# Expert shares from one tanh, routing in smaller pieces, ten gather buffers, and a different order of softmax steps in a decoder layer on one core

## The reference

```python
x = x + attn(layernorm(x), ...)            # 16 heads of 16, rotary, layernorm of q and k
x = x + xattn(layernorm(x), ctx, ...)      # 16 heads, low-rank queries, latent context of 64
x = x + ffn(layernorm(x), Wr, Wg, Wu, Wd)

def ffn(x, Wr, Wg, Wu, Wd):                # 8 experts of width 256, the best 2 for each token
    probs = softmax(x @ Wr)
    topk_w, topk_idx = top_k(probs, 2)
    topk_w = topk_w / sum(topk_w)
    return sum over experts i of w_i * ((silu(x @ Wg[i]) * (x @ Wu[i])) @ Wd[i])
```

## Time and profile before

| what | value |
|---|---|
| timed runs, median | 677.04 us |
| profiled execution, its own time | 674.06 us |
| its span | 672.3 us |
| PE busy, share of the span | 601.7 us, 89% |
| DVE busy | 498.5 us, 74% |
| ACT busy | 339.6 us, 51% |
| POOL busy | 250.2 us, 37% |
| chain that ended last, by engine | PE 66%, DVE 18%, ACT 9%, issue 4%, DMA 3% |

### The profile page before, as it was taken

One profiled execution on the slowest core, in us unless ns is written; L12 is line 12 of the kernel. 1 busy time (PEld: TensorE's weight loads), 2 busy tenths in 40 slices (PEclk: granted clock), 3 DMA queues, 4 the chain that ended last, 5 costly groups with the idle time before them and its releaser, 6 DMA issues.

```text
span 672.3 us, 14930 instructions
## 1 busy us (share of the span) xinstructions
PE 601.7 (89%) x5522; PEld 452.4 (67%) x5522; DVE 498.5 (74%) x1197; ACT 339.6 (51%) x1178; POOL 250.2 (37%) x226
## 2 busy tenths in 40 slices
PE   2786989998899999999999999999988888899980
PEld 1465777777778766676766766767655677788860
DVE  3899799998366797737987489874798877655574
ACT  1277899999573024741157212671238735455540
POOL 2104000000003853833447734667346413734330
PEclk9897999998799999999999999999997999999995
DMA  8599990000000000000000120002127212433366
GB/s 285 167 338 338 335 319 3 2 2 1 1 2 17 17 0 3 2 1 17 1 1 2 64 63 1 2 1 71 42 81 235 64 48 78 145 108 98 112 217 221
DMA packets 40679, 58.96 MB, mean 88 GB/s; under 512 B 15040, under 2 KB 35136, under 8 KB 39968
## 3 DMA queue, kind: packets, MB, share of 16 engines
q1 hardware_dynamic: 35536, 47.25, 22.8%
q0 software_dynamic: 3408, 9.34, 3.8%
q10 hardware_dynamic: 1664, 1.41, 0.7%
HBM read 46.56 MB, written 29.40 MB: 113 GB/s over the span
## 4 chain that ended last, share of the span: by engine, by line
PE 66%; DVE 18%; ACT 9%; issue 4%; DMA 3%; ACTq 0%; SPq 0%; DVEq 0%
PE bank L378 57%; PE bank L387 9%; ACT ex L1640 2%; ACT kbd L1630 2%; DVE x L1552 2%; DMA lncol<-in_L_attn_ln_kv_b 1%; DVE nmax L1064 1%; DMA gb<-results 1%; DVE wlo L1486 1%; DVE m L1163 1%; DVE yr L1026 1%; DVE hvar L1031 1%; ACT ex L1750 1%; DVE newton L1045 1%; DVE newton L1047 1%
## 5 line engine op out<-in xcount | busy, mean ns | idle before, releaser
L1898 POOL TENSOR_TENSOR r<-m,m 128x512 f32<-128x512 f32 x80 | 104.5, 1331 | 101.6 <-DVE m L1163 87.7
L1163 DVE TENSOR_TENSOR m<-bank,cst 128x512 f32<-128x512 f32 x192 | 122.1, 685 | 25.7 <-PE bank L378 21.0
L1750 ACT ACTIVATE ex<-bank,nmax 128x64 f32<-128x64 f32 x256 | 73.4, 341 | 27.7 <-DVE nmax L1452 27.7
L378 PE MATMUL bank<-xth,wbh 128*128 128x512 f32 x192 | 80.0, 417 | 0.0
L378 PE MATMUL bank<-xth,wbl 128*128 128x512 f32 x192 | 75.3, 392 | 0.0
L378 PE MATMUL bank<-xtl,wbh 128*128 128x512 f32 x192 | 75.0, 390 | 0.0
L1733 ACT ACTIVATE qc<-bank 128x512 f32<-128x512 f32 x32 | 17.4, 595 | 98.8 <-PE bank L378 98.8
L378 PE MATMUL bank<-wop,qc 128*128 128x256 f32 x256 | 62.3, 389 | 0.0
L1945 POOL DMA_INDIRECT results<-ys,place x39 | 37.9, 971 | 62.5 <-ACT ys L1825 60.7
L378 PEld LDWEIGHTS bank<-wop,qc 128*128 128x128 f32 x256 | 46.6, 189 | 14.7 <-issue 8.1
L1640 ACT ACTIVATE ex<-bank,nmax 128x64 f32<-128x64 f32 x256 | 54.5, 358 | 2.6 <-DVE nmax L1064 2.5
(11 more groups left out here) (245 smaller groups left out, 1420.7 us busy)
## 6 DMA issues: line engine op xcount, KB each, us to landing
slots<-in_fill SPq DMA_DIRECT2D x1, 17544.0 KB, 65.2
xs<-slots SPq DMA_DIRECT2D x39, 129.0 KB, 2.2
gb<-results SPq DMA_DIRECT2D x16, 256.0 KB, 3.7
wo_s<-in_L_xattn_Wo SPq DMA_DIRECT2D x1, 2048.0 KB, 18.6
wq_s<-in_L_xattn_Wq SPq DMA_DIRECT2D x1, 2048.0 KB, 11.9
wraw<-in_L_ffn_Wg SPq DMA_DIRECT2D x8, 256.0 KB, 3.8
wraw<-in_L_ffn_Wu SPq DMA_DIRECT2D x8, 256.0 KB, 4.0
wraw<-in_L_ffn_Wd SPq DMA_DIRECT2D x8, 256.0 KB, 4.6
```

The lines of the kernel that those rows point to most:

```text
L378: return e.matmul(o, l, r, start=start, stop=stop, skip_group_check=True)
L1163: last = e.tensor_tensor(m4[n % 2][m][:, :].rearrange("p (b s) -> p b s", s=S), products[half][:, :].rearrange("p (b s) -> p b s", s=S), t ...
L1750: last = e.activation(ex[b % 4][:, h * 64:(h + 1) * 64], score_banks(b)[odd][:, n * 64:(n + 1) * 64], ACT.Exp, bias=nmax[b % 4][:, 4 * odd ...
L1898: last = e.tensor_tensor(rope[n % 6][half][:, :], m4[n % 2][first][:, :], m4[n % 2][second][:, :], op)
```

## The change

1. **Shares.** The exponential of the logits is gone. Ranking compares the logits less their maximum, which DVE has made already. `rank_chosen` keeps of the second-best expert that difference (`behind`, a column for each tile of tokens), and `rank_shares` is gone. In step 14 of the experts ACT computes one tanh for all 16 tiles, and DVE makes both shares of it in step 15 (`shares`).
2. **Smaller pieces.** In the expert steps, `rank_compare`, `rank_sum` and `rank_chosen` of block 3 stand in steps 3, 4 and 5, the slots in step 7 (6 before), the scatters one tile later, and the table's work, in steps 7 and 8 before, in steps 8 to 12. The signal for the rows comes in step 11, the one for the experts in step 12.
3. **Gathering.** Ten buffers in place of four: SP loads tiles 0 to 11 in six pairs (512 KB each) without waiting for sums, and tiles 12 to 15 singly. DVE adds one tile in each step from 36 on, its two sums apart. Tile 12 is scaled by ACT and added by POOL. ACT issues four of the seven output DMAs.
4. **Softmax order.** In steps 4 to 6: `contexts` half 0, `cross_scores`, `contexts` half 1, `cross_weights_T`.

```diff
-        ROUTE_LAST = {"stats": -1, "norm": 0, "T": 1, "logits": 2, "max": 2, "exp": 3, "rank": 4, "pos": 6, "slots": 6}
-        LAST_SCATTERS = {5: (0, 1), 6: (2, 3), 7: (4, 5), 8: (6, 7)}
-        COMBINES = {EARLY_DONE + n: c for n, c in ((5, (0, 1)), (6, (2, 3)), (7, (4, 5)), (8, (6, 7, 8)), (9, (9, 10, 11)))}
+        ROUTE_LAST = {"stats": -1, "norm": 0, "T": 1, "logits": 2, "max": 2, "rank": 3, "pos": 6, "slots": 7}
+        TANH_AT = 14
+        LAST_SCATTERS = {6: (0, 1), 7: (2, 3), 8: (4, 5), 9: (6, 7)}
+        COMBINE_FROM = EARLY_DONE + 5
+        SUMMED_APART = 4 * EARLY
...
                     if 4 <= s < 7:
+                        contexts(blk, s - 4, (0,))
                         cross_scores(blk, s)
-                        contexts(blk, s - 4, (0,))
+                        contexts(blk, s - 4, (1,))
                         cross_weights_T(blk, s - 3)
-                        contexts(blk, s - 4, (1,))
...
-                e.scalar_tensor_tensor(ew[:, :, :], rank[:, :, :], 2.0, ew[:, :, :], ALU.is_lt, ALU.mult).then_inc(r_route, 1)
+                e.scalar_tensor_tensor(pick[1][:, :, :], rank[:, :, :], 1.0, ew[:, :, :], ALU.is_equal, ALU.mult).then_inc(r_route, 1)
                 w.wait_ge(r_route, at + 10)
                 e.tensor_tensor(before[:, 1, :], before[:, 0, :], chosen[:, 0, :], ALU.add)
-                e.tensor_reduce(esum[:, :], ew[:, :, :], AX, ALU.add).then_inc(r_route, 1)
...
+                e.tensor_reduce(behind[:, 4 * b:4 * b + 4], pick[1][:, :, :], AX, ALU.add).then_inc(r_route, 1)
+                for t in range(1, 4):
+                    w.wait_ge(r_route, at + 10 + t)
+                    e.tensor_tensor(before[:, t + 1, :], before[:, t, :], chosen[:, t, :], ALU.add).then_inc(r_route, 1)
+
+            def shares():
+
+                w.wait_ge(r_tanh, 1)
+                for k, sign in enumerate((-0.5, 0.5)):
+                    e.tensor_scalar(share[:, :, k], behind[:, :], sign, 0.5, ALU.mult, ALU.add).then_inc(r_shares, 1)
...
+                if i >= COMBINE_FROM:
+                    combine(i - COMBINE_FROM, 0)
                 if i + 2 < tiles:
                     x_low(i + 2)
                 if i + 2 < tiles:
                     places(i + 2)
+                if i >= COMBINE_FROM:
+                    combine(i - COMBINE_FROM, 1)
                 route_step(3, i, ROUTE_LAST)
...
-                for t in COMBINES.get(i, ()):
-                    combine(t)
-            for t in range(4 * EARLY, NT):
-                combine(t)
+            for t in range(tiles + 2 - COMBINE_FROM, NT):
+                if t != SUMMED_APART:
+                    for k in range(2):
+                        combine(t, k)
...
-                elif n == at["exp"]:
-                    w.wait_ge(r_route, RK * b + 5)
-                    e.activation(ew[:, :, :], ew[:, :, :], ACT.Exp).then_inc(r_exp, 1)
...
+                if i == TANH_AT:
+                    w.wait_ge(r_route, RK * 3 + 11)
+                    e.activation(behind[:, :], behind[:, :], ACT.Tanh, scale=0.5).then_inc(r_tanh, 1)
+            w.wait_ge(t_comb, 16)
+            e.dma_start(ov[:, 4:8, :], x3[:, 4:8, :]).then_inc(d_out, 16)
+            t = SUMMED_APART
+            for k in range(2):
+                w.wait_ge(r_shares, 2)
+                w.wait_ge(d_gb[GB_OF[t][0]], 16)
+                part = gb[GB_OF[t][0]][:, 0, k, :]
+                e.activation(part, part, ACT.Copy, scale=share[:, t, k:k + 1]).then_inc(t_scaled, 1)
+            w.wait_ge(t_comb, 24)
+            e.dma_start(ov[:, 8:12, :], x3[:, 8:12, :]).then_inc(d_out, 16)
+            for t in (13, 15):
+                w.wait_ge(t_comb, 2 * combined(t + 1))
+                e.dma_start(ov[:, t:t + 1, :], x3[:, t:t + 1, :]).then_inc(d_out, 16)
...
+            t = SUMMED_APART
+            for k in range(2):
+                w.wait_ge(t_scaled, k + 1)
+                w.wait_ge(t_summed, k)
+                e.tensor_tensor(tile(t), tile(t), gb[GB_OF[t][0]][:, 0, k, :], ALU.add).then_inc(t_summed, 1)
...
-            for t in range(8):
-                results_load(t)
+            for t in range(0, 4 * EARLY, 2):
+                results_load(t, t + 2)
+            w.wait_ge(t_comb, 8)
             result(0, 4)
-            for t in range(8, 12):
-                results_load(t)
-            result(4, 8)
-            result(8, 12)
-            for t in range(12, NT):
-                results_load(t)
-            for t in range(12, NT):
-                result(t, t + 1)
+            for t in range(4 * EARLY, NT):
+                results_load(t, t + 1)
+            w.wait_ge(t_summed, 2)
+            result(SUMMED_APART, SUMMED_APART + 1)
+            w.wait_ge(t_comb, 2 * combined(15))
+            result(14, 15)
```

More of the change, by code:

```diff
@@ L230, in decoder @@
         emax = s4("emax", [P, 4])
-        esum = s4("esum", [P, 4])
+        behind = s4("behind", [P, NT])
         rank = s4("rank", [P, 4, E])
@@ L308, in decoder @@
         ys = [s7(f"ys{i}", [P, D]) for i in range(YS)]
-        gb = [s7(f"gb{i}", [P, 2, D]) for i in range(4)]
+        pairs = [s7(f"gb{i}", [P, 2, 2, D]) for i in range(5)]
         assert s7.at <= after_scores
+        pairs.append(Space(nc, mxhat_at)("gb5", [P, 2, 2, D]))
+        s8 = Space(nc, low.at)
+        ones = [s8(f"gb{i}", [P, 1, 2, D]) for i in range(6, 9)]
+        ones.append(Space(nc, mxT_at)("gb9", [P, 1, 2, D]))
+        gb = pairs + ones
+        GB_OF = {t: (t // 2, t % 2) for t in range(4 * EARLY)}
+        GB_OF.update({t: (2 * EARLY + t - 4 * EARLY, 0) for t in range(4 * EARLY, NT)})
         slots = nc.dram_tensor("slots", (ROWS, D + 2), F32, kind="Internal").ap()
@@ L318, in decoder @@
         d_fill, d_scat = sem("d_fill"), sem("d_scat")
-        d_xs, d_ys, d_gb = ([sem(f"d_{n}{i}") for i in range(k)] for n, k in (("xs", 4), ("ys", YS), ("gb", 4)))
+        d_xs, d_ys, d_gb = ([sem(f"d_{n}{i}") for i in range(k)] for n, k in (("xs", 4), ("ys", YS), ("gb", 10)))
         s_phase = sem("phase")
@@ L1381, in late_ends @@
                 past_of(TILES[1], 2 * E)
-            def late_rows():
-                n, cols = TILES[1], slice(COLS[1], COLS[1] + TILES[1])
-                mine = slice(FIRST[1], FIRST[1] + n)
-                w.wait_ge(r_tab, TAB + 7)
-                e.tensor_scalar(own[:, mine], C("iota"), float(P), C("part"), ALU.mult, ALU.add)
-                e.tensor_tensor(pastnext[:, :, :], past[:, :, :], in_tiles(C("next"), n), ALU.mult)
-                e.tensor_tensor(pastgap[:, :, :], past[:, :, :], in_tiles(gap[:, :], n), ALU.mult).then_inc(r_tab, 1)
-                w.wait_ge(r_tab, TAB + 8)
-                e.tensor_reduce(expert[:, :], pastnext[:, :, :], AX, ALU.add)
-                e.tensor_reduce(rowf[:, :], pastgap[:, :, :], AX, ALU.add).then_inc(r_tab, 1)
+            late = slice(FIRST[1], FIRST[1] + TILES[1])
@@ new lines, in vector, with late_gaps @@
+            late_cols = slice(COLS[1], COLS[1] + TILES[1])
+            def late_gaps():
+                w.wait_ge(r_tab, TAB + 7)
+                e.tensor_scalar(own[:, late], C("iota"), float(P), C("part"), ALU.mult, ALU.add)
+                e.tensor_tensor(pastgap[:, :, :], past[:, :, :], in_tiles(gap[:, :], TILES[1]), ALU.mult).then_inc(r_tab, 1)
+                w.wait_ge(r_tab, TAB + 8)
+                e.tensor_reduce(rowf[:, :], pastgap[:, :, :], AX, ALU.add).then_inc(r_tab, 1)
+            def late_rows():
@@ L1393, in late_rows @@
                 w.wait_ge(r_tab, TAB + 9)
-                e.tensor_scalar(eoff[:, cols], expert[:, :], float(WE), None, ALU.mult)
-                e.scalar_tensor_tensor(own[:, mine], rowf[:, :], starts[:, 0:1], own[:, mine], ALU.add, ALU.add)
-                e.scalar_tensor_tensor(row[:, cols], rowf[:, :], starts[:, 0:1], C("fill"), ALU.add, ALU.add).then_inc(r_tab, 1)
+                e.scalar_tensor_tensor(own[:, late], rowf[:, :], starts[:, 0:1], own[:, late], ALU.add, ALU.add)
+                e.scalar_tensor_tensor(row[:, late_cols], rowf[:, :], starts[:, 0:1], C("fill"), ALU.add, ALU.add).then_inc(r_tab, 1)
@@ L1397, in late_rows, with late_experts @@
                 w.wait_ge(r_tab, TAB + 10)
+                e.drain().then_inc(r_table, 1)
+                e.tensor_tensor(pastnext[:, :, :], past[:, :, :], in_tiles(C("next"), TILES[1]), ALU.mult).then_inc(r_tab, 1)
+            def late_experts():
+                w.wait_ge(r_tab, TAB + 11)
+                e.tensor_reduce(expert[:, :], pastnext[:, :, :], AX, ALU.add).then_inc(r_tab, 1)
+                w.wait_ge(r_tab, TAB + 12)
+                e.tensor_scalar(eoff[:, late_cols], expert[:, :], float(WE), None, ALU.mult).then_inc(r_tab, 1)
+                w.wait_ge(r_tab, TAB + 13)
@@ L1546, in h_low, with combine @@
                                 ALU.subtract).then_inc(t_hl, 1)
-            def combine(t):
-                for k in range(2):
-                    w.wait_ge(d_gb[t % 4], 16 * (t // 4 + 1))
```

(8 more changed lines are left out.)

78 lines of the change are left out of this document (39 added, 39 removed).

## The result

The changed kernel took **671.27 us** (median of 4 runs, 670.39 to 671.77) beside 677.15 for the kernel before in the same session (4 runs, 676.82 to 677.63): a ratio of 0.991, 95% interval 0.9895 to 0.9921. It is 5.9 us faster, where 10.3 were forecast: the right side, inside the range by 0.2 us, and 4.6 us above the forecast of 666.7. Its profiled execution took 671.66 us for a span of 669.8. (One later execution of the kernel before took 1977 us and is left out of every comparison.)

A forecast was written before the change was run, and what follows sets the result against it. No single limit was taken to bound the kernel: TensorE in blocks 0 to 2, mutual waits in block 3, DVE's sums at the end. Cross-attention -1.4, expert steps -4.2, tail -4.7 gave -10.3, from 677.04 to 666.7 us, range 661.5 to 671.5.

The forecast's parts named there:

- blocks 0 to 2: Softmax phases of cross-attention: new order gains 0.35 us a step, less added waits: 1.85 us, bounds 0.4 and 5.6.
- block 3: Last cross-attention block: scores come about 2 us later behind `qc`; 0.65 lost, bounds 0 and 2; shorter ranking returns 0.2.
- tile 17: Expert step 15: PE waits 0.6 us for the load behind the last scatter and `place`'s wait, bounds 0 and 2.
- steps 3 to 12: Expert steps: removed table loads and smaller DVE pieces cut 28.61 us to 23.81, a gain of 4.80 us.
- The wait that the order adds: Softmax step 6: first half waits for ACT's copy, about 0.8 us in block 0, 0.25 taken in blocks 1 and 2.
- Table loads: On ACT: two in all remain; the tanh takes about 0.2 us with no table load beside it.
- The tail: DVE's sums at the end: gather waits and tile 12's sums go, GpSimd costs 1.1; -4.7 us, bounds -6.5 and -2.
- Rival 1: Tail: last gathers land 3 us late and DVE waits for tile 13 again; -7.3 us, 669.7 us; chance 0.15.
- The slower rival: Expert steps: lower clock persists from block 3; five such steps eat the 10.3 us, six give 682 us; chance 0.04.

The follow-up runs named there:

- the order alone: The kernel before with the new softmax order of steps 4 to 6 in all four blocks and nothing else: 670.44 us, ratio 0.9994.
- the last run: Changed kernel with old softmax order in block 3 and tile 12 summed on DVE, repeated unchanged on a fourth chip: 661.42 us, ratio 0.9844.
- the two kernels with moved scatters: Changed kernel, old order in block 3, tile 12 on DVE; scatters 2, 1, 2, 1, 2 over steps 6 to 10 (663.61 us) or pairs two steps later (667.32).
- tile 12 on DVE: Changed kernel with old softmax order in block 3 and tile 12 summed by two more DVE instructions: 666.55 us, again on another chip 661.42 us.
- Spreading the issues: Changed kernel with old softmax order in block 3 and one scatter a step in steps 6 to 13: 673.71 us, ratio 0.9953.
- the three with moved scatters: Changed kernel, old order in block 3: one scatter a step (673.71 us); with tile 12 on DVE also, scatters 2, 1, 2, 1, 2 (663.61) or two steps later (667.32).
- scatters 2, 1, 2, 1, 2: Changed kernel, old order in block 3, tile 12 on DVE, eight scatters as 2, 1, 2, 1, 2 over steps 6 to 10: 663.61 us, ratio 0.988.

## Why the prediction was right in sign and 4.6 us too low

Microseconds by part. Second column: the two kernels profiled again on one chip with late signals. Third: profiles without them, each part from the kernels named behind the table.

| part | forecast | late signals | none late |
|---|---|---|---|
| ahead of cross-attention (not changed) | 0 | -0.7 | - |
| blocks 0 to 2 (`kvT` to `slot`) | -1.85 | -3.0 | -2.5 |
| block 3 (`slot` to first `gated`) | +0.45 | +3.5 | +1.3 |
| steps 3 to 14 | -4.8 | -3.1 | -5.1 |
| tile 17 (steps 14 to 16) | +0.6 | +0.2 | +1.6 |
| step 16 to the last sum | -4.7 | -5.7 | -5.4 |
| behind the last sum | 0 | +1.2 | +1.2 |
| sum | -10.3 | -7.5 | -8.9 |

The third column compares the first profile of before with the order alone (blocks), with the last run (steps, tile 17), and for the tail with that run less the 0.49 us of tile 12; its 1.2 us behind the last sum are those of the second column. The changed kernel itself was not run on such a chip, so -8.9 is worked out, not measured. The second adds up to its spans, 676.3 and 668.8; the medians of that session differ by 5.7, so single profiles are good to about 2 us in sum and far better within a stage. Against the forecast, block 3 is 3.1 us worse in the second column, steps 3 to 14 are 1.7 and the end 1.2; the other parts are 3.2 better together. In the third column misses of both signs cancel (block 3, tile 17 and the end 3.1 worse, the others 1.7 better), so that -8.9 comes near -10.3 is in part luck.

- **The mechanisms of steps 3 to 12 were right, and so was the size (4.80 forecast, 28.61 - 23.73 = 4.88 found), where TensorE's signals come in time.** In the first result they don't, and the faster steps meet the scatters with more stall: 7.1 to 8.4 us above 12.7 in steps 8 to 13, the lower clock included, where the kernel before had 17.81 - 13.11 = 4.7. So the first step that failed is this: I took the stages of one profile as those of the timed runs, and let the 3 us between them stand as a constant. The profile (674.06) shows no late signal; the timed runs of that session (677.04) are like those of the chips that have them. That the 3 us were a stall in the very steps that the change speeds up fits this, but those timed runs have no trace that shows it.
- **Block 3 is the second step that failed, and the largest miss**: 0.65 of 2.0 us were taken, 1.3 to 3.5 are lost. The scores do come behind the wait for `qc`, as forecast: PE stands for 2.19 us at 510.16 and 1.07 at 514.83. But I counted one delay of 2.0 us, and there are two. DVE's maxima of the scores of steps 5 and 6 show them, in the order alone first, then in the changed kernel:

```profile
509.12 0.69 DVE L1452 TENSOR_REDUCE nmax<-bank 128x8 f32<-128x512 f32 x1 [1.92 <-PE bank L378]
512.68 0.69 DVE L1452 TENSOR_REDUCE nmax<-bank 128x8 f32<-128x512 f32 x1 [1.48 <-PE bank L378]
```
```profile
512.60 0.69 DVE L1473 TENSOR_REDUCE nmax<-bank 128x8 f32<-128x512 f32 x1 [2.59 <-PE bank L395]
518.23 0.69 DVE L1473 TENSOR_REDUCE nmax<-bank 128x8 f32<-128x512 f32 x1 [3.55 <-remote]
```

   Measured from `slot`, in the kernel before they stand 6.22 and 8.92 us behind it, in the order alone 8.22 and 11.78: 2.00 and 2.86 late, since PE, DVE and ACT wait for each other in turn and the second delay adds to the first. By the last maximum of the block 1.32 us are left, and they reach the first `gated`. So some of it is absorbed, 1.5 of 2.86, but less than the two thirds that I took. In the changed kernel the two are 2.67 and 5.60 us late, of which 3.38 reach the first `gated`. The second pair are 5.63 us apart, the first 3.56: here too a late signal, beside scatters of block 2's routing, adds 2 us.
- **Blocks 0 to 2** gained 2.5 to 3.0 us, within the bounds; step 4 took 1.83 us in place of 2.23. The wait that the order adds ahead of step 6 is there as forecast: 0.69, 0.32 and 0.32 us in blocks 0, 1 and 2 of the order alone (0.8, 0.25 and 0.25 taken). A wait of 0.42 us for `qc` in block 0 goes, for which I had no term. The shorter ranking gives little: the order alone takes 262.40 us from `kvT` to `slot`, and the two kernels with moved scatters, which have the shorter ranking as well, 262.12 and 261.95 on the same chip. The Trainium skill ("TensorEngine Tiling (Array Packing)", Key Properties) puts a drain on every change of the tiling mode; by its drains alone the term would have been 0.4 us, and the blocks measured 2.5 or more, so the half that sits beside the scores does gain of its own.
- **Table loads**: the second load of the program is that of the experts at 541.10, 1.28 us; the tanh at 591.01 takes 0.22 us with none beside it, as forecast.
- **The tail** gained 5.4 to 5.7 where 4.7 were forecast, in part since GpSimd stretched only two sums by 0.35 and 0.28 us over 0.48, not by 1.1 in all. Against it stand 1.2 us behind the last sum, GpSimd's drain, for which I had no term. Rival 1, late gathers, did not come.
- **Tile 17** cost 1.6 us where nothing else was late (0.6 taken, bounds 0 and 2), and nothing where the stall covered it.
- **The slower rival**: the granted clock fell to 0.50, the lower level of 1.2 GHz, from about 503 to 507 and 510 to 514, and again in the stall from 578 to 585. It never held through the steps, so the kernel did not become slower, but it is about 2.2 us of the stall.

## What to carry to other kernels

A profile that is faster than the timed runs is not a scaled copy of them: profile the kernel twice, on two chips if possible, before a gain is put into the stage that might hold the difference. In a stage where PE, DVE and ACT wait for each other in turn, waits put into one of them add up (here 1.3 of 2.9 us reached the end of the stage, and 3.4 of 5.6 with late signals); try a reordering there apart from the dense blocks. The version with the old order in block 3 and tile 12 on DVE has a ratio to the kernel before of 0.9854 and 0.9844 on the two kinds of chip; the changed kernel has 0.991 on the slower kind and was not run on the other.

## What the runs showed of the hardware

- **Chips (or sessions: there was one for each chip) differ in the same kernel by 0.9%**: 676.9 and 676.7 us on two chips, 671.1 and 671.6 on two others for the kernel before, 666.5 and 661.4 for the best version, with granted clocks of 0.95 to 0.97 on all of them. The difference sits where GpSimd issues indirect DMAs back to back: on the slower kind ACT and DVE start up to 6 us behind TensorE's records there, and in the four profiles of the faster kind they never do. Every execution on record comes with a span and a granted clock; whether the stall is there when nothing is recorded, no run shows.
- Spreading the issues took 4.3 of the 7.1 us away, so the issues (or the packets behind them) seem to take part in it; it is one run. For a part of the late signals the semaphore records settle that TensorE had done its work: in the changed kernel the updates of `gate_up`, `h_T`, `down` and `x_T` stand at 581.60, 581.64, 581.72 and 581.76, and the same four stand 1.15 us apart from first to last in the last run (576.73 to 577.88), where nothing is late. The Trainium skill ("Perfetto Trace Analysis", Per-instruction lifecycle) says that waits for semaphores and their propagation lie outside the window that a record brackets, which fits.
- The traces with late signals also hold fewer semaphore updates. For one and the same program (tile 12 on DVE) they are 4808 on the slower chip and 5468 on the faster. Why, stays open.
- A sum on DVE that began 0.22 us into an addition on GpSimd took 0.83 us in place of 0.48. Two additions of 1.64 us together delayed DVE by 0.63. The Trainium skill ("SBUF — State Buffer", SBUF: two separate sides) calls the shared port pair an exclusive lock for the whole instruction; by that the sum should have waited out the 0.56 us left of the addition and ended after 1.04. The measurement is a delay, and not the whole one; but spans on GpSimd are rough in a profile, so how long it held the ports is not shown.
- GpSimd's drain at the end of its program took 6.64 us behind tile 12's additions, and 7.20 and 8.10 behind a last store (tile 12 on DVE; kernel before).
- The last scatter took 2.7 us from issue to landing, the load behind it 2.1 us, and 0.6 us of register work lay between them on SP. From the chain that ended last in the run with scatters 2, 1, 2, 1, 2 (start, length, what; us):

```profile
577.55 2.72 DMA slots<-mxhat,index
...
580.36 0.63 SPq L380
...
581.16 2.09 DMA xs<-slots
```

   From the start of the last scatter's issue to the first use of its rows it took 5.75, 6.23, 5.66 and 5.66 us in the four runs in which PE waited for them (the three with moved scatters and the last run).
